# A decoder layer's expert stage: the shared expert's groups eight blocks apart instead of nine

## The reference

```
def _swiglu_mlp(x, wg, wu, wd):
    return jax.nn.silu(x @ wg) * (x @ wu) @ wd
...
scores = jax.nn.softmax(logits, axis=-1)
topk_w, topk_i = jax.lax.top_k(scores, K)              # K = 2 of E = 8 experts
...
y = jnp.einsum('te,etd->td', combine, expert_out)      # F = 176
return y + _swiglu_mlp(identity, sw_gate, sw_up, sw_down)   # the shared expert, 352 wide
...
x = _layernorm(x + _L0_ffn_ref(x, ...), axis=-1)
```

## Time and profile before

| | |
|---|---|
| median of the runs | 1994.52 us (1994.47 to 1996.31) |
| the profiled execution's own time | 2005.11 us |
| its span | 2003.3 us |
| mean granted clock of TensorE over the span | 0.991 |
| busy: PE, DVE, ACT, POOL | 97%, 75%, 64%, 64% |
| instructions of the span | 47354 |
| chain that ended last | PE 15% of the span is named, among it e_ps_y L2006 3%, e_ps_s L2033 2%, e_ps_h L1998 2% |
| first transpose of a block | 1643.18 us |
| last scatter issued | 1977.55 us |

### The profile page before, as it was taken

One profiled execution on the slowest core, in us unless ns is written; L12 is line 12 of the kernel. 1 busy time (PEld: TensorE's weight loads), 2 busy tenths in 40 slices (PEclk: granted clock), 3 DMA queues, 4 the chain that ended last, 5 costly groups with the idle time before them and its releaser, 6 DMA issues. The chain is left out here.

```text
span 2003.3 us, 47354 instructions
## 1 busy us (share of the span) xinstructions
PE 1945.2 (97%) x15995; PEld 1680.5 (84%) x15995; DVE 1495.3 (75%) x3905; ACT 1277.9 (64%) x3925; POOL 1288.6 (64%) x1461
## 2 busy tenths in 40 slices
PE   8999989999999999999999999999999988999997
PEld 4555579999999999999999998999999877888875
DVE  6999966777777777777777778777777755655665
ACT  5777666666666666666666666666666654555565
POOL 6888875666666666666666666666666654444664
PEclk9999989999999999999999999999999998999999
DMA  6101000000000000000000001000000011222454
GB/s 172 40 19 30 19 17 9 12 16 16 15 23 14 19 15 16 14 23 16 17 16 15 17 20 35 17 16 16 15 22 11 11 45 57 86 86 80 127 147 142
DMA packets 103984, 75.27 MB, mean 38 GB/s; under 512 B 10998, under 2 KB 97638, under 8 KB 103622
## 3 DMA queue, kind: packets, MB, share of 16 engines
q1 hardware_dynamic: 94806, 54.20, 9.7%
q0 software_dynamic: 8640, 17.97, 2.5%
q10 hardware_dynamic: 304, 0.07, 0.1%
HBM read 39.64 MB, written 32.57 MB: 36 GB/s over the span
## 5 line engine op out<-in xcount | busy, mean ns | idle before, releaser
L1213 POOL TENSOR_TENSOR x_prob<-x_prob,x_inv 128x496 f32<-128x496 f32 x512 | 520.7, 1017 | 454.2 <-DVE x_inv L1334 451.5
L1278 ACT ACTIVATE x_prob<-x_ps_S,x_nmax 128x248 f32<-128x248 f32 x1024 | 472.1, 468 | 225.7 <-DVE x_nmax L1328 223.8
L1328 DVE TENSOR_REDUCE x_nmax<-x_ps_S 128x2 f32<-128x496 f32 x512 | 343.1, 670 | 102.0 <-PE x_ps_S L1084 93.9
L1293 ACT COPY x_probT<-x_ps_T 124x512 f32<-124x512 f32 x512 | 300.8, 588 | 165.8 <-PE x_ps_T L1480 163.6
L1082 PE MATMUL x_ps_S<-first_kT_lo,x_G_hi 128*128 128x248 f32 x1024 | 326.8, 319 | 0.0
L1480 PE MATMUL x_ps_T<-ident,x_prob 128*124 128x128 f32 x2048 | 318.7, 278 | 6.2 <-POOL x_prob L1213 4.8
L1480 PEld LDWEIGHTS x_ps_T<-ident,x_prob 128*124 128x124 f32 x2048 | 232.7, 140 | 72.5 <-POOL x_prob L1213 28.8
L1084 PE MATMUL x_ps_S<-first_kT_hi,x_G_hi 128*128 128x248 f32 x1024 | 283.8, 277 | 0.0
L1083 PE MATMUL x_ps_S<-first_kT_hi,x_G_lo 128*128 128x248 f32 x1024 | 283.7, 277 | 0.0
L1450 PE MATMUL x_ps_O<-x_probT,x_V 124*64 124x128 f32 x4096 | 252.4, 276 | 0.7 <-issue 0.7
L1314 DVE TENSOR_TENSOR x_G_lo<-x_ps_G,x_G_hi 128x512 fp32r<-128x512 f32 x256 | 176.1, 688 | 88.4 <-ACT x_G_hi L1272 88.3
(11 more groups left out here) (267 smaller groups left out, 4421.8 us busy)
## 6 DMA issues: line engine op xcount, KB each, us to landing
w_wkv<-sorted_rows SPq DMA_DIRECT2D x142, 66.0 KB
e_back<-sorted_results SPq DMA_DIRECT2D x32, 256.0 KB
latents<-first_nlat SPq DMA_DIRECT2D x32, 128.0 KB, 1.8
turned_rows<-w_rows SPq DMA_DIRECT2D x32, 128.0 KB, 1.8
w_wq<-turned_rows SPq DMA_DIRECT2D x32, 128.0 KB
out_dram<-e_result SPq DMA_DIRECT2D x16, 256.0 KB
first_nk<-latents SPq DMA_DIRECT2D x32, 124.0 KB
first_nk<-in_ctx SPq DMA_DIRECT2D x32, 120.0 KB, 2.2
```

What stands on the lines that cost most here:

```text
L1213: nc.gpsimd.tensor_tensor(prob[:, k], prob[:, k], inv[:, k].unsqueeze(2).broadcast_to([P, 2, K]), ALU.mult).then_inc(prob_ready, 1)
L1278: nc.scalar.activation(prob[:, k, h, :], ps_S[:, n % BANKS, h * K:(h + 1) * K], ACT.Exp, bias=nmax[:, k, h:h + 1], accum_out=total[:, k, h ...
L1293: nc.scalar.copy(probT[0:KT, s % (2 * GANG)], ps_T[0:KT, s % 2, :]).then_inc(probT_ready, 1)
L1328: nc.vector.tensor_reduce(nmax[:, k, :], ps_S[:, n % BANKS, 0:2 * K].rearrange("p (h k) -> p h k", h=2), AX, ALU.max, negate=True).then_in ...
```

## The change

EVERY, the distance between groups' starts, is 8 instead of 9, the constants for a late last group go, and shared_at has one rule for all groups. Only the step without a piece behind the third one is left. Group g now stands at steps 8 + 8g to 15 + 8g, group 15 at 128 to 135.

```
     SHARED_FROM = 8
-    EVERY = 9
-    LATE = 1
-    LATE_FROM = TOTAL + 1
+    EVERY = 8
...
         def shared_at(t):
 
-            if t >= LATE_FROM:
-                g, k = divmod(t - LATE_FROM, PIECES)
-                g += GROUPS - LATE
-            else:
-                g, k = divmod(t - SHARED_FROM, EVERY)
-                if g >= GROUPS - LATE or k in (NS, EVERY - 1):
-                    return None, None
-                k -= k > NS
+            g, k = divmod(t - SHARED_FROM, EVERY)
+            if k == NS:
+                return None, None
+            k -= k > NS
             return (g, k) if 0 <= g < GROUPS else (None, None)
```

## The result

The changed kernel is slower: 2004.20 us (median of five, 2003.92 to 2007.14) against 1994.47 (median of five, 1993.26 to 1996.31), a ratio of 1.0051, 95% interval [1.004, 1.0063], or +9.7 us. Forecast were +5.5 us and a range of 1994.8 to 2004.9.

A forecast was written before the change was run, and what follows sets the result against it. PE was taken as the bound mid-stage, but not over blocks 99 to 134 or after the last block. +9.9 us at block 135, -5.4 to the last scatter and +1.0 behind it gave +5.5, 2000.0 us; range 1994.8 to 2004.9.

The forecast's parts named there:

- PE-paced case: Rival, block 135 to last scatter: GpSimd keeps up, scatter out after 14.0 us instead of 18.1; +1.4, 1995.9 us; chance 0.18.
- long low clock: Rival, adds behind the last scatter: over 9 us at 1.2 GHz give +7.2, 2001.7 us; chance 0.12.
- To block 99: Loop up to block 99: the new kernel has done a group and two gate and up pieces more, +9.6 us.
- Blocks 99 to 134: These 36 steps: 79.7 us undisturbed plus 6.0 of stalls after the change, against 85.4 before.
- Last stretch: Block 135 to the last scatter: GpSimd's scatters set the pace, 18.1 us for 23.5, giving back 5.4 us.
- Behind the last scatter: Adds of returned rows after the last scatter: PE idles some 10 us, then runs at low clock, +1.0 us.
- pricing of bare steps: Block 135 to last scatter: PE needs 1.40 us per bare step, so its scatter would be out after 14.0 us.
- rival of vanishing collisions: Rival, blocks 99 to 134: stalls may vanish without the ninth step; 6.0 us off, -0.5, 1994.0 us; chance 0.10.

The follow-up runs named there:

- ahead14: The changed kernel with the work on the returned rows of groups 0 to 9 two steps later (AHEAD 14 for 12): 2002.06 us, ratio 1.0037.
- base: The kernel before, unchanged, profiled a second time: 1993.91 us.
- light_pool: The changed kernel with most of GpSimd's add_pair of group 9 and the roots of groups 8 and 9 left out: 2002.88 us, ratio 1.0037.
- late22: The kernel before with spacing 8, groups 0 to 14 at steps 22 to 141, group 15 still behind block 141: 1991.01 us, ratio 0.9983.
- late8: The kernel before with groups 0 to 14 eight steps apart instead of nine, group 15 still behind block 141: 2002.86 us, ratio 1.0037.
- from14: The changed kernel with its groups begun at step 14 instead of 8 (SHARED_FROM): 1995.95 us, ratio 1.0004.

## Why the prediction was right, and its size too small

The direction and the range held, the range narrowly: 2004.20 lies 0.7 us below its end, and 0.5 below what the forecast's own bounds add up to (its upper ones give +10.2 us, 2004.7 and not 2004.9; a microsecond below the PE-paced case is 1994.9 and not 1994.8). The nearest case on paper was the long low clock with 9 us of stalls, 2004.7. That is chance: the low clock lasted 5.4 us and the stalls were 6.4. What brought the time there are four misses in one direction. Against the measured stretches:

- *To block 99*, +9.6 us forecast, +10.7 measured. The counting of pieces is right in the middle, where groups repeat every 17.97 us (forecast 18.0). The rest, 1.1 us, arises between blocks 16 and 32, which took 38.9 us for 36.5; two down pieces more explain 1.2 of these 2.4. I had taken nothing for the work beside the table; what collides there was not tried and stays open.
- *Blocks 99 to 134*, +0.3 forecast, +2.3 measured. The new time was right (85.7 forecast, 86.1), by stalls of 6.4 us for 6.0. The collisions are those that were named: the steps behind all_lo and add_back (102, 110, 118 and 126) took 2.55 us each, the bare ones (107, 115, 123 and 131) 2.31 to 2.39, together 5.0 us of the 6.4. In ahead14 the same steps took 1.94 to 2.20 and 1.61 to 1.68. The term failed at its other side: 85.36 us of the earlier trace rows came from the longer first profile, in base the kernel before takes 83.8.
- *Last stretch*, -5.4 forecast, -4.2 measured; the new one took 18.9 for 18.1. The forecast had GpSimd set the pace, and it did keep it: from block 132's scatter to 141's passed 15.9 us for 15.4, and GpSimd was idle in between for only 0.3 us more, ahead of block 137's, than it is between scatters that stand back to back. What failed is the bound behind it: the forecast let PE pass a bare step in 1.40 us and have the last scatter out after 14.0. With most of GpSimd's other work taken out (light_pool) the stretch still took 17.8, so GpSimd was worth 1.0 us. A bare step takes 1.4 to 1.5 us only behind long steps and without returned rows; in a row it took 1.6 at the start of late22. With returned rows it took 1.9, singly in base and in a row in the changed kernel, and 2.1 in late8.
- *Behind the last scatter*, +1.0 forecast, +1.4 measured. The mechanism was right: 1.8 us by the clock, less what a shorter wait for group 11's rows gives.

GpSimd's scatters of blocks 132, 137 and 141 in the changed kernel:

```profile
1958.98 0.96 POOL L1743 DMA_INDIRECT sorted_results<-e_y,w_wkv  x1 [1.14 <-DVE e_y L1877]
...
1968.54 0.95 POOL L1743 DMA_INDIRECT sorted_results<-e_y,w_wkv  x1 [0.61 <-DVE e_y L1877]
...
1974.86 0.96 POOL L1743 DMA_INDIRECT sorted_results<-e_y,w_wkv  x1 [0.30 <-issue]
```

The forecast's summary, that group 15's later pieces "ran while the scatter landed and cost nothing, and is now paid for in the loop", counted PE's work right and named the wrong culprit. late8 leaves group 15 in its covered place, and its last scatter is still 9.0 us late, as late as the changed kernel's (8.9). The weakest step is the pricing of bare steps: the 14 that stood singly behind the groups, 1.58 us each in base, stand at the end in late8 at 2.11; in the changed kernel six of them are left, at 1.91 where it can be measured, and the steps before them are filled with group 15. The rival "paced by PE at the end" priced them at 1.40 too, and was wrong for that reason: PE's side needed 17.8 us and not 14.0. The rival of vanishing collisions is refuted by the 6.4 us; base had 6.1 in the same blocks, so collisions are hardly a part of the difference. from14 and ahead14 show what it takes to lose them, another phase. The long low clock lasted 5.4 us, not 9.

The price of a matmul at the low clock was 1.8 times the full one in the forecast, from the earlier trace rows. Group 10's add lay wholly at the low clock; VectorE's sum followed its start (1980.76) after 3.82 us in the changed kernel

```profile
1984.58 0.69 DVE L1912 TENSOR_TENSOR e_hsum<-e_ps_gu,X 128x512 f32<-128x512 f32 x1 [11.18 <-PE e_ps_gu L2038]
```

and after 2.03 us in base (1971.74 to 1973.77), a factor of 1.88. Both times hold what does not follow PE's clock, such as the way to VectorE, so the factor of the products alone is larger still. By the Trainium skill (TensorE: Matmul & The Clock Gate, "Wait — 56ns, not 53.3ns?") it is 1.98 for 512 columns. These rows are nearer to the page's factor than to the forecast's.

## What to carry to other kernels

A pipeline step that is empty on the bound engine is only as cheap as the other engines' chain for a block lets it be: here 1.4 to 1.5 us between full steps, 1.6 in a row, and about 1.9 wherever returned rows had to be handled beside it. So spread fillers to the end of the loop, and put the empty steps where the other engines have the least to do. When two rhythms share the in-order queues of ScalarE and VectorE, try their phases before their rates; two steps of shift took 4.2 us of stalls away here. And profile the kernel before twice when its profiled time stands apart from its median.

## What was not expected of the hardware

- The same kernel took 1994.3 to 1994.7 us on three chips and 2004.6 and 2005.1 us on two others, as much as the whole effect; only ratios on one chip can be compared.
- The granted clock fell to 0.50 in late8, for over 6 us of full work, though PE had not stood idle for more than 0.94 us at a time just before. In the changed kernel it fell in 7.69 us of idleness.
- Normalising two sequences on ScalarE took 0.67 us for 4 columns and 0.87 for 128: cutting its width took little away.
